# Edge attributes as three bf16 terms, in 24 one-pass products per step

## The chip, the cores and the metric

The kernel runs on one core of one Trainium2 chip. The metric is the device time of one execution in microseconds. A core has five engines that run their own instruction streams and meet only at semaphores: PE (TensorE, matrix products into the PSUM memory), DVE (VectorE), ACT (ScalarE), POOL (GpSimd) and SP (SyncE, which here only issues transfers). Transfers move on DMA queues: POOL issues the indirect ones (gathers of rows by index), SP and ACT the plain ones.

## The reference, cut to what matters

Four graph layers over 6,250 nodes with 96 features and 206,250 edges, sorted by destination. Every edge has 32 attributes. The two layers in the middle use them:

```python
# layer 1 (sum over the edges of a node)
msg = jax.nn.relu(x[src] + edge_attr @ We + be)
aggr = jax.ops.segment_sum(msg, dst, num_segments=x.shape[0])
...
# layer 2, twice (maximum over the edges of a node)
msg = x[src] @ W_msg + edge_attr @ W_edge
agg = jax.ops.segment_max(msg, dst, num_segments=x.shape[0])
return agg + x @ W_root + b
```

Layer 0 is an attention over edges in the other order (sorted by source), layer 3 an attention over the edges in the given order. Neither uses the attributes. All inputs are float32.

## The kernel before, in words

The program is a row of blocks, one after the other. A preparation block sorts and builds tables and loads the weights. Block `e0` is the attention stage of layer 0: 416 chunks of 512 edges. Three edge passes follow, all written by the same function `edge_pass`: `e1` (sum), `e2a` and `e2b` (maximum). Block `e3` is the attention of layer 3, 404 chunks of 512 edges in batches of four. Short node blocks stand between them.

**An edge pass** has 202 steps (`NS`), each of 1,024 edges that stand as 128 rows of 8 edges. For a step s:

- SP loads the attributes (`load_attr`, L1117), 128 rows of 256 float32: two blocks of 128 columns, four edges' 32 attributes each above one another on the rows. Four buffers (`RA`), so it runs four steps ahead; a load waits until PE is done with the buffer (`t_attr`). In even steps it loads masks, and then it stores the result of two steps earlier (L1126).
- POOL gathers the features of the 8 source nodes of each row by 8 indirect transfers (L1151) into one of three buffers. The gathers of step s + 3 wait until the `add` of step s has read its buffer (`v_add`).
- PE makes `edge_attr @ W` by two float32 products (L1168). The attributes are the operand that is held in the array (128x128), and the moving one is a 128x384 matrix with the 32x96 weight four times on its diagonal. Two PSUM buffers `EA`: the products of step s wait for the `add` of step s - 2. Every fourth step, PE also makes a transpose (L1166 in `e1`) or a product (L1164 in `e2a`, `e2b`) for one of the 49 node tiles, the "root" work.
- DVE waits for the products (`t_attr`) and the gathered rows and adds them (L1187), then transposes (L1193), runs three segmented scans (L1202) and transposes back (L1210). In `e1` ACT applies the relu (L1227) before the first transpose.

The last instruction of PE's step raises `t_attr`. Two instructions wait on it: DVE's `add(s)` and SP's attribute load of step s + 4.

**The attention stage `e0`**, per chunk: SP reads four row numbers from memory and issues four window loads (L766, L767), and stores an older chunk's result (L759). POOL makes four gathers (L789). DVE multiplies and reduces to scores (L877, L880), clips (L883), scans (L845) and multiplies by the weights (L894). ACT builds the selection matrices (L911, L914), takes the exponentials (L962, L964) and copies the result out of PSUM (L905). PE makes four float32 products for the queries (L805) and two groups of four transposes (L829, L812). The order of all of this is written out in the source, chunk by chunk.

## Time and profile before

| | |
|---|---|
| time, median of 3 executions | 13151.55 us (13120.66 to 13181.02) |
| span of the profiled execution, first to last instruction | 13179.5 us |
| that execution's own time, the highest of the three | 13181.02 us |
| PE busy, weight loads beside it | 4527.1 us (34%), 3022.1 us (23%) |
| DVE busy | 6535.8 us (50%) |
| ACT busy | 1994.5 us (15%) |
| POOL busy | 8151.7 us (62%) |
| attention stage `e0` | about 640 to 3,430 us |
| edge passes `e1`, `e2a`, `e2b` | about 3,440 to 5,712, 5,845 to 8,110, 8,210 to 10,480 us |
| attention `e3` | about 10,640 to 13,060 us |
| granted TensorE clock, mean | 0.541 of 2.4 GHz |

The table says how long each engine was at work, not who set the pace: no engine is busy for more than 62% of the span. That is read stage by stage, from what each engine waits for. Two things help to read the rows below. A float32 product stands in the trace as two MATMUL rows and two LDWEIGHTS rows (202 steps of two products give 808 of each). And the profile notes when a matrix product starts; its end is modelled. A wait that it puts down to "remote" or "issue" has no releaser that it could find.

### The profile page before, as it was taken

The numbers are of one execution on the slowest core, as the hardware profiler recorded it, in microseconds if no ns is written. First come the engines' busy times: TensorE is split into PE (matmuls) and PEld (weight loads), VectorE is DVE, ScalarE is ACT, GpSimd is POOL, SyncE is SP. The second block draws the span as 40 slices with busy tenths as digits, with TensorE's granted clock in tenths as the row PEclk, the third lists the DMA queues.
The fourth block names the chain that finished last, engine by engine and source line by source line (L and its number), as shares of the span: only waits on it lengthen the run. The fifth ranks groups of instructions, "written<-read, shape, count | busy, mean of one in ns | idle before, by whom it ended". The sixth has DMA issues, their size and how long they took to land. (4 is left out here: it accounts for less than half of the span.)

```text
span 13179.5 us, 81573 instructions
## 1 busy us (share of the span) xinstructions
PE 4527.1 (34%) x15877; PEld 3022.1 (23%) x15877; DVE 6535.8 (50%) x10237; ACT 1994.5 (15%) x4360; POOL 8151.7 (62%) x8551
## 2 busy tenths in 40 slices
PE   3354455555222222232222222222222234434443
PEld 3244344444110111111111111111111123333332
DVE  9543344444544454454445455444544544444445
ACT  3233333333100000010000000000000022222223
POOL 1455555555676666656666666766666666666665
PEclk7555555555555555555555555555555555555555
DMA  2355555555333333323333332333333222222222
GB/s 76 106 155 154 149 152 155 153 159 152 99 86 82 87 89 87 88 72 85 87 87 93 81 91 79 87 85 88 89 87 86 81 58 66 69 68 68 68 69 63
DMA packets 1007936, 1264.02 MB, mean 96 GB/s; under 512 B 483123, under 2 KB 740467, under 8 KB 1007331
## 3 DMA queue, kind: packets, MB, share of 16 engines
q0 software_dynamic: 303696, 520.91, 17.5%
q1 hardware_dynamic: 638139, 635.93, 14.8%
q10 hardware_dynamic: 65600, 101.96, 2.7%
q8 instruction: 136, 2.23, 0.1%
q14 instruction: 365, 2.99, 0.1%
HBM read 829.46 MB, written 428.44 MB: 95 GB/s over the span
## 5 line engine op out<-in xcount | busy, mean ns | idle before, releaser
L789 POOL DMA_INDIRECT e_got<-kv_tab,dst_cols x1661 | 1574.5, 948 | 1281.7 <-DVE e_pay L894 770.2
L1843 POOL DMA_INDIRECT e_got<-h_tab,src_tcols x1612 | 1540.9, 956 | 881.8 <-issue 473.8
L1151 POOL DMA_INDIRECT e2a_got<-x_tab,src_cols x1616 | 1531.3, 948 | 775.7 <-issue 556.2
L1151 POOL DMA_INDIRECT e_got<-x_tab,src_cols x1616 | 1553.5, 961 | 718.3 <-issue 586.9
L1151 POOL DMA_INDIRECT e2b_got<-x_tab,src_cols x1616 | 1531.3, 948 | 745.7 <-issue 518.8
L1168 PE MATMUL e2b_EA<-we_W_edge,e2b_attr 128*128 128x384 f32 x808 | 574.9, 866 | 1331.2 <-DVE e2b_emsg L1187 728.3
L1168 PE MATMUL e_EA<-we_We,e_attr 128*128 128x384 f32 x808 | 578.3, 871 | 1297.8 <-issue 898.1
L1168 PE MATMUL e2a_EA<-we_W_edge,e2a_attr 128*128 128x384 f32 x808 | 572.0, 862 | 1300.4 <-issue 767.3
L894 DVE TENSOR_TENSOR e_pay<-e_got,e_Q 128x384 f32<-128x384 f32 x416 | 230.2, 553 | 1570.4 <-ACT e_Q L962 1129.1
L1940 DVE TENSOR_TENSOR_SCAN e_run<-e_Z,e_run,e_msg 98x512 f32<-98x512 f32 x404 | 516.9, 1279 | 795.4 <-ACT e_msg L2005 619.8
L805 PE MATMUL e_Q<-e_window,e_pick 128*128 128x96 f32 x3328 | 758.9, 408 | 79.1 <-issue 41.2
L805 PEld LDWEIGHTS e_Q<-e_window,e_pick 128*128 128x128 f32 x3328 | 744.0, 327 | 84.8 <-issue 82.8
L812 PE MATMUL e_B<-ident,e_run 100*128 100x100 f32 x1664 | 374.5, 379 | 904.4 <-issue 493.3
L1854 PE MATMUL e_B<-ident,e_run 98*128 98x98 f32 x1616 | 357.1, 374 | 759.2 <-DVE e_run L1940 627.7
L1168 PEld LDWEIGHTS e2b_EA<-we_W_edge,e2b_attr 128*128 128x128 f32 x808 | 236.8, 323 | 1621.6 <-issue 1620.1
L829 PE MATMUL e_M<-ident,e_pay 128*100 128x128 f32 x1664 | 445.8, 422 | 470.0 <-DVE e_pay L894 366.4
L1168 PEld LDWEIGHTS e_EA<-we_We,e_attr 128*128 128x128 f32 x808 | 239.7, 327 | 1590.5 <-issue 1590.2
L1168 PEld LDWEIGHTS e2a_EA<-we_W_edge,e2a_attr 128*128 128x128 f32 x808 | 235.8, 321 | 1589.1 <-issue 1587.1
L845 DVE TENSOR_TENSOR_SCAN e_run<-e_keep,e_run,e_M 100x512 f32<-100x512 bf16 x416 | 532.3, 1280 | 11.5 <-issue 7.2
L1187 DVE TENSOR_TENSOR e2a_emsg<-e2a_EA,e2a_got 128x768 f32<-128x768 f32 x202 | 191.9, 950 | 692.4 <-remote 458.4
L1187 DVE TENSOR_TENSOR e2b_emsg<-e2b_EA,e2b_got 128x768 f32<-128x768 f32 x202 | 192.1, 951 | 671.5 <-remote 396.5
L1187 DVE TENSOR_TENSOR e_emsg<-e_EA,e_got 128x768 f32<-128x768 f32 x202 | 192.7, 954 | 648.3 <-remote 529.4
(373 smaller groups left out, 10316.0 us busy)
## 6 DMA issues: line engine op xcount, KB each, us to landing
scan_out<-e_out SPq DMA_DIRECT2D x416, 200.0 KB
e_window<-q_tab SPq DMA_DIRECT2D x1664, 48.0 KB
scan_out<-e_out SPq DMA_DIRECT2D x404, 196.0 KB
scan_out<-e_out SPq DMA_DIRECT2D x202, 384.0 KB
scan_out<-e2a_out SPq DMA_DIRECT2D x202, 384.0 KB
scan_out<-e2b_out SPq DMA_DIRECT2D x202, 384.0 KB
e_rel<-rel_row ACTq DMA_DIRECT2D x208, 256.0 KB
e_keep<-keep_row ACTq DMA_DIRECT2D x208, 200.0 KB
```

The costliest lines, as they stand in the source:

```text
L789: e.indirect_dma_start(got[i][:, k, :], None, kv_tab, bass.IndirectOffsetOnAxis(dst_c[:, c * K + k:c * K + k + 1], axis=0)).then_inc(s_g[i ...
L805: ins = e.matmul(Q[c % 3][:, k * D:(k + 1) * D], pick[c % 4][:, k, :], window[c % U][:, k, :], start=True, stop=True)
L812: ins = e.transpose(B[c % 2][:, k * PAY:(k + 1) * PAY], run[c % 3][:, k::K], ident[0:PAY, 0:PAY])
L829: ins = e.transpose(M[c % 3][0:PAY, k * P:(k + 1) * P], pay[c % 4][:, k, :], ident[:, :])
L845: e.tensor_tensor_scan(run[c % 3][:, :], keep[c // 2 % KR][:, at:at + CH], M[c % 3][0:PAY, :], run[(c + 2) % 3][:, CH - 1:CH], ALU.mult, A ...
L894: e.tensor_tensor(pay[c % 4][:, :, 0:D].rearrange("p k (h d) -> p k h d", h=HEADS), got[c % RG0][:, :, D:2 * D].rearrange("p k (h d) -> p ...
L1151: e.indirect_dma_start(got[s % RS][:, k, :], None, x_tab, bass.IndirectOffsetOnAxis(src_cols[:, q:q + 1], axis=0)).then_inc(edge_got[s % R ...
L1168: ins = e.matmul(EA[s % 2][:, h, 0:K * D], attr[s % RA][:, h * P:(h + 1) * P], edge_w[:, :], start=True, stop=True)
L1187: e.tensor_tensor(emsg[s % 3][:, :, :].rearrange("p (h k) d -> p h (k d)", h=2), EA[s % 2][:, :, 0:K * D], got[s % RS][:, :, :].rearrange( ...
L1843: e.indirect_dma_start(got[c % RG][:, k, :], None, h_tab, bass.IndirectOffsetOnAxis(src_tcols[:, q:q + 1], axis=0)).then_inc(s_g[c % RG], 16)
L1854: ins = e.transpose(B[v % 2][:, k * HW:(k + 1) * HW], run[v % 2][:, k::K], ident[0:HW, 0:HW])
L1940: V[v].give(e.tensor_tensor_scan(run[p][:, :], Z[p][0:HW, :], msg[p][:, :], run[q][:, CH - 1:CH], ALU.mult, ALU.add), "scan")
```

## The change

The attributes no longer stand as float32. In the attention stage `e0`, which does not use them, every batch of four steps' attributes (128 rows of 1,024) is loaded, split into three bf16 terms and stored in a table `attr_terms` in memory: the value rounded to bf16, the rest rounded to bf16, and the rest of that. The three add up to the float32 value. There are 51 batches, one every 8 chunks. SP loads a batch (L796) at chunk 2 of the eight, ACT rounds at chunks 3 and 5 (L1014, L1019), DVE subtracts at chunks 4 and 7 (L917, L922), SP stores the three terms at chunk 14 (three transfers, L802).

In the edge passes SP loads, for a step, the three terms one above the other: 96 rows of 1,024 bf16. The weights are split in the same way in the preparation block, each term standing three times on 96 rows. For each of a step's eight 128-edge columns, PE multiplies the same 96x128 attributes with the three terms of the weight and sums in PSUM. These are all nine pairs of terms. So a step's two float32 products with 384 moving columns become 24 bf16 products with 96 (L1254).

```diff
-        we = {n: keepb("we_" + n, [P, K * D]) for n in ("We", "W1_edge", "W2_edge")}
+        we = {n: keepb("we_" + n, [3 * DE, 3, D], BF16) for n in ("We", "W1_edge", "W2_edge")}
...
-                    e.wait_ge(p_set, 1 + len(we))
...
-                    for n in we:
-                        e.memset(we[n][:, :], 0.0).then_inc(p_set, 1)
...
+                    e.wait_ge(s_w, 16 * len(loads))
+                    for n in we:
+                        e.tensor_copy(we[n][:, 0, :], edge_f[n][:, :]).then_inc(p_edge, 1)
+                    e.wait_ge(p_edge, 3)
+                    for n in we:
+                        e.tensor_tensor(edge_f[n][:, :], edge_f[n][:, :], we[n][:, 0, :], ALU.subtract).then_inc(p_edge, 1)
...
+            SPLIT_AT, SPLIT_STEP = 2, 8
...
+                    def load_attr(b):
+                        n = split_rows(b)
+                        after(e, v_term, 2 * (b - 1))
+                        e.dma_start(attr_f[b % 2][0:n, :], t["attr_S"][b * P:b * P + n, :]).then_inc(s_af[b % 2], 16)
+
+                    def store_terms(b):
+                        n = split_rows(b)
+                        e.wait_ge(v_term, 2 * b + 2)
+                        for i in range(3):
+                            e.dma_start(attr_terms[b, i, 0:n, :], attr_t[b % 2][0:n, i, :]).then_inc(s_at[b % 2], 16)
...
+                    def rest(b):
+                        n = split_rows(b)
+                        e.wait_ge(a_term, 2 * b + 1)
+                        e.tensor_tensor(attr_f[b % 2][0:n, :], attr_f[b % 2][0:n, :], attr_t[b % 2][0:n, 0, :], ALU.subtract).then_inc(v_term, 1)
...
+                    def first_term(b):
+                        n = split_rows(b)
+                        e.wait_ge(s_af[b % 2], 16 * (b // 2 + 1))
+                        after(e, s_at[b % 2], 48 * (b // 2))
+                        e.activation(attr_t[b % 2][0:n, 0, :], attr_f[b % 2][0:n, :], ACT.Copy).then_inc(a_term, 1)
...
-                attr = [ph.sb(f"attr{i}", [P, 2 * P]) for i in range(RA)]
+                attr = [ph.sb(f"attr{i}", [3 * DE, 2 * K * P], BF16) for i in range(RA)]
...
                         def load_attr(s):
                             after(e, t_attr, s - RA + 1)
-                            e.dma_start(attr[s % RA][:, :], t["attr_S"][s]).then_inc(s_attr[s % RA], 16)
+                            lo = s % SPB * DE
+                            e.dma_start(attr[s % RA][:, :], attr_terms[s // SPB, :, lo:lo + DE, :]).then_inc(s_attr[s % RA], 16)
...
-                            for h in range(2):
-                                ins = e.matmul(EA[s % 2][:, h, 0:K * D], attr[s % RA][:, h * P:(h + 1) * P], edge_w[:, :], start=True, stop=True)
+                            for k in range(2 * K):
+                                for j in range(3):
+                                    ins = e.matmul(EA[s % 2][:, k // K, k % K * D:(k % K + 1) * D], attr[s % RA][:, k * P:(k + 1) * P], edge_w[:, j, :],
+                                                   start=j == 0, stop=j == 2)
                             ins.then_inc(t_attr, 1)
```

The order that stands in the built programs shows two places. The first is PE in the pass `e1`, one root step and the step behind it (`e_attr` are the attributes, `we_We` the weight). Before:

```order
L1166 MATMUL e_EA<-ident,X 96x128 [waits edge_v_pick,edge_v_add,edge_attr0]
L1168 MATMUL e_EA<-we_We,e_attr 128x384 x2
L1168 MATMUL e_EA<-we_We,e_attr 128x384 [waits edge_v_add,edge_attr1]
L1168 MATMUL e_EA<-we_We,e_attr 128x384
L1168 MATMUL e_EA<-we_We,e_attr 128x384 [waits edge_v_add,edge_attr2]
L1168 MATMUL e_EA<-we_We,e_attr 128x384
```

After:

```order
L1251 MATMUL e_EA<-ident,X 96x128 [waits edge_v_pick,edge_v_add,edge_attr0]
L1254 MATMUL e_EA<-we_We,e_attr 128x96 x24
L1254 MATMUL e_EA<-we_We,e_attr 128x96 [waits edge_v_add,edge_attr1]
L1254 MATMUL e_EA<-we_We,e_attr 128x96 x23
L1254 MATMUL e_EA<-we_We,e_attr 128x96 [waits edge_v_add,edge_attr2]
L1254 MATMUL e_EA<-we_We,e_attr 128x96 x23
```

The waits stand where they stood; a step has 24 instructions for 2.

The second place is SP in the attention stage, at a chunk where the terms of a batch are stored (`e_window` are the query rows, `R` holds a term). After:

```order
L810 DMA e_window<-q_tab 128x96
L791 DMA scan_out<-e_out 128x400 [waits edge_a_out]
L802 DMA attr_terms<-R 128x1024 [waits e0_g_v_term]
L802 DMA attr_terms<-R 128x1024 x2
L809 TENSOR_LOAD first_row [waits edge_t_q]
L809 ISA x2
```

Before:

```order
L767 DMA e_window<-q_tab 128x96
L759 DMA scan_out<-e_out 128x400 [waits edge_a_out]
L766 TENSOR_LOAD first_row [waits edge_t_q]
L766 ISA x2
```

Three stores, the first with a wait for DVE's last subtraction, now stand behind the store of a chunk and ahead of the next chunk's windows.

## Rows read from the trace of the kernel before

**Rows 1.** Windows of four stages; columns in the header row.
```profile
core 0: us, PE busy (x) PEld busy (x) DVE busy (x) ACT busy (x) POOL busy (x), PEclk, DMA share, GB/s
640.00:3430.00 2790.00, 1391.47 (x6270) 1204.76 (x6269) 1245.60 (x2061) 882.92 (x2143) 1560.32 (x1643) 0.51 0.55 151
3440.00:5712.00 2272.00, 588.77 (x857) 241.25 (x857) 1120.52 (x1258) 169.45 (x201) 1553.52 (x1616) 0.54 0.32 87
10640.00:13060.00 2420.00, 984.29 (x5376) 762.65 (x5377) 1143.52 (x2900) 620.95 (x1296) 1535.80 (x1608) 0.54 0.26 68
```

**Rows 2.** Source view of L1187, first pass: duration ns, first and last start.
```profile
L1187 DVE TENSOR_TENSOR e_emsg<-e_EA,e_got x202: 915/957/959, 3452.0 to 5711.5; 128x768 f32<-128x768 f32 x101
```

**Rows 3.** Costliest groups of the page (line, engine, names, busy, mean ns, idle, releaser).
```profile
L1151 POOL DMA_INDIRECT e_got<-x_tab,src_cols x1616 | 1553.5, 961 | 718.3 <-issue 586.9
L1168 PE MATMUL e_EA<-we_We,e_attr 128*128 128x384 f32 x808 | 578.3, 871 | 1297.8 <-issue 898.1
L1187 DVE TENSOR_TENSOR e_emsg<-e_EA,e_got 128x768 f32<-128x768 f32 x202 | 192.7, 954 | 648.3 <-remote 529.4
```

**Rows 4.** Timeline at 3494 us: start, duration, engine, line, operation, idle before.
```profile
3494.31 2.90 PE L1168 MATMUL e_EA<-we_We,e_attr 128*128 128x384 f32 x4 [8.55 <-issue]
3497.24 0.33 SPq L1117 DMA_DIRECT2D e_attr<-in_attr_S  x1
3501.66 0.96 DVE L1187 TENSOR_TENSOR e_emsg<-e_EA,e_got 128x768 f32<-128x768 f32 x1 [1.96 <-DMA e_got<-x_tab,src_cols]
```

**Rows 5.** Timeline at 4400 us, same pass.
```profile
4400.15 2.90 PE L1168 MATMUL e_EA<-we_We,e_attr 128*128 128x384 f32 x4 [8.28 <-issue]
...
4411.64 0.33 SPq L1117 DMA_DIRECT2D e_attr<-in_attr_S  x1
...
4413.07 0.94 POOL L1151 DMA_INDIRECT e_got<-x_tab,src_cols  x1 [3.11 <-issue]
...
4422.82 0.35 SPq L1117 DMA_DIRECT2D e_attr<-in_attr_S  x1
4422.83 0.96 DVE L1187 TENSOR_TENSOR e_emsg<-e_EA,e_got 128x768 f32<-128x768 f32 x1 [4.49 <-remote]
```

**Rows 6.** Timeline at 6420 us, second pass.
```profile
6420.26 0.33 SPq L1117 DMA_DIRECT2D e2a_attr<-in_attr_S  x1
...
6421.32 0.71 PE L1164 MATMUL e2a_EA<-Wrc,xT_all 96*128 96x96 f32 x2 [8.25 <-issue]
...
6431.46 0.35 SPq L1117 DMA_DIRECT2D e2a_attr<-in_attr_S  x1
...
6447.56 0.33 SPq L1117 DMA_DIRECT2D e2a_attr<-in_attr_S  x1
```

**Rows 7.** Timeline at 11580 us, attention over the ordered edges.
```profile
11576.14 1.06 PE L1868 MATMUL e_M<-ident,e_emsg 128*98 128x128 f32 x4
...
11584.15 0.94 POOL L1843 DMA_INDIRECT e_got<-h_tab,src_tcols  x1 [0.30 <-issue]
11587.67 0.60 ACT L2005 ACTIVATE e_msg<-e_M 98x512 f32<-98x512 f32 x1 [7.53 <-remote]
...
11589.34 0.95 POOL L1843 DMA_INDIRECT e_got<-h_tab,src_tcols  x1 [4.24 <-ACT e_hold L2017]
```

**Rows 8.** Timeline at 1490 us, first attention stage, SP's queue and POOL.
```profile
1486.81 10.37 SPq L767 DMA_DIRECT2D e_window<-q_tab  x4
...
1503.11 0.94 POOL L789 DMA_INDIRECT e_got<-kv_tab,dst_cols  x1 [8.20 <-DVE e_pay L894]
```

**Rows 9.** All groups by line: a bf16 product, and what bears on the split.
```profile
L1864 PE MATMUL e_Z<-e_parts,e_sel 80*98 80x128 bf16 x1616 | 252.2, 308 | 113.3 <-issue 74.0 <-DVE e_mid L1979 25.4 <-DVE e_parts L1981 10.5
L894 DVE TENSOR_TENSOR e_pay<-e_got,e_Q 128x384 f32<-128x384 f32 x416 | 230.2, 553 | 1570.4 <-ACT e_Q L962 1129.1 <-issue 440.8
L1227 ACT ACTIVATE e_emsg<-e_emsg 128x768 f32<-128x768 f32 x202 | 170.3, 843 | 2108.4 <-issue 1571.1 <-DVE e_emsg L1187 537.3
L647 DVE TENSOR_TENSOR prep_A<-prep_A 128x1024 f32<-128x1024 f32 x49 | 60.0, 1225 | 1.7
```

More of the change, by code:

```diff
@@ L147, in build @@
     neg_row = scratch("neg_row", (EP,), BF16)
+    SPB = P // DE
+    NAB = -(-(NCH // 2) // SPB)
+    attr_terms = scratch("attr_terms", (NAB, 3, P, 2 * K * P), BF16)
     ad_row = scratch("ad_row", (EP,))
@@ L335, in build @@
             assert NCH <= 512 and G * CH <= NT * D and NG <= PB
+            edge_f = {n: ph.sb("edge_f_" + n, [3 * DE, D]) for n in we}
+            p_edge = ph.sem("p_edge")
             loads = [(src_cols[:, 0:NCH * K], t["src_cols"]), (src_tcols[:, 0:NTL], t["src_tcols"])]
@@ L346, in build @@
             for n, key in (("We", "L1_gnn_We"), ("W1_edge", "L2_gnn_W1_edge"), ("W2_edge", "L2_gnn_W2_edge")):
-                for k in range(K):
-                    loads.append((we[n][k * DE:(k + 1) * DE, k * D:(k + 1) * D], t[key]))
+                for i in range(3):
+                    loads.append((edge_f[n][i * DE:(i + 1) * DE, :], t[key]))
             def pairs(buf, lo, n, y):
@@ L729, in build, with split_of, split_rows @@
             s_dst, v_keep, s_kept = pf.sem("dst"), pf.sem("keep"), pf.sem("st")
+            EW = 2 * K * P
+            assert 7 * EW // 2 <= NT * D
+            R_flat = R[:, :, :].rearrange("p t d -> p (t d)")
+            attr_f = [R_flat[:, i * EW:(i + 1) * EW] for i in range(2)]
+            attr_t = [R_flat[:, 2 * EW:7 * EW // 2].bitcast(BF16).rearrange("p (i n) -> p i n", i=3),
+                      pf.sb("attr_t1", [P, 3, EW], BF16)]
+            s_af, s_at = [ph.sem(f"g_af{i}") for i in range(2)], [ph.sem(f"g_at{i}") for i in range(2)]
+            a_term, v_term = ph.sem("g_a_term"), ph.sem("g_v_term")
+            SPLIT_AT, SPLIT_STEP = 2, 8
+            assert SPLIT_AT + SPLIT_STEP * (NAB - 1) + 12 < NCH0
+            def split_of(c, at):
+                b, r = divmod(c - SPLIT_AT - at, SPLIT_STEP)
+                return b if r == 0 and 0 <= b < NAB else None
+            def split_rows(b):
+                return min(P, NCH // 2 * DE - b * P)
             v_half, t_first, a_first, a_le, a_row, a_cnt, v_end = (pf.sem(n) for n in ("ld", "pe", "first", "le", "row", "cnt", "f"))
@@ L759, in store @@
                         e.dma_start(out_c[c], out[c % U][:, :, :].rearrange("p k d -> p (k d)")).then_inc(s_st[c % U], 16)
+                    def load_attr(b):
[5 more added lines that the diff above has]
+                        e.wait_ge(v_term, 2 * b + 2)
+                        for i in range(3):
+                            e.dma_start(attr_terms[b, i, 0:n, :], attr_t[b % 2][0:n, i, :]).then_inc(s_at[b % 2], 16)
                     BEHIND = 13
@@ L769, in _ @@
                             store(c - BEHIND)
+                        b = split_of(c, 0)
+                        if b is not None:
+                            load_attr(b)
+                        b = split_of(c, 12)
+                        if b is not None:
+                            store_terms(b)
                         if c == U - 1:
@@ L779, in _ @@
                     e.wait_ge(s_kept, 32)
+                    for i in range(2):
+                        e.wait_ge(s_at[i], 48 * len(range(i, NAB, 2)))
                     for u in range(U):
@@ L891, in _ @@
                             ends()
+                        b = split_of(c, 2)
+                        if b is not None:
+                            rest(b)
+                        b = split_of(c, 5)
+                        if b is not None:
+                            last_term(b)
                         e.wait_ge(a_exp, c + 1)
@@ L972, in _ @@
                             keep_in((c + 4) // 2)
+                        b = split_of(c, 1)
+                        if b is not None:
+                            first_term(b)
+                        b = split_of(c, 3)
+                        if b is not None:
+                            second_term(b)
                         if ROWS_AT <= c < ROWS_AT + NT:
```

17 lines of the change are left out of this document (16 added, 1 removed).

## The prediction, on record before the result

> **What bounds the kernel now.** I read the windows by stage first. In an edge pass no engine is full: DVE is busy for 1,120.5 of 2,272 us, POOL for 1,553.5, PE for 588.8 beside 241.3 of weight loads [rows 1]. So something waits. The source view of L1187, the addition at the head of DVE's step, gives the pace: 202 of them between 3452.0 and 5711.5 us [rows 2], 11.24 us a step. The other two passes have nearly the same length.
>
> POOL alone could go faster. A gather is 0.94 us, with 0.30 us of gap before it [rows 7], so eight take 10.0 us. DVE alone could go much faster: 1,120.5 / 202 is 5.5 us. In the page's costliest groups DVE idles 648 us before its addition, and the profile puts 529 of them down to "remote"; POOL idles 718 us [rows 3].
>
> The timeline tells who it is. Early in the pass (rows at 3494 us) a step's four MATMUL rows start at 3494.31 and last 2.90 us, and SP's attribute load, which waits for `t_attr` alone, starts at 3497.24: PE's word comes at once, and the addition waits for the gather until 3501.66 [rows 4]. Nine hundred microseconds later it is otherwise. The products of the step whose addition starts at 4422.83 stand in the trace at 4400.15, for 2.90 us. SP's load, which waits for the same `t_attr`, starts at 4422.82, within 0.01 us of the addition [rows 5]. At 4411.64 the load of the step before did the same. What DVE and SP have in common is `t_attr`, so the word of PE comes 19.8 us after the modelled end of its products. POOL is held by it in turn: it had been idle for 3.11 us at 4413.07 [rows 5]. **The late release by PE sets the pace of the edge passes**, and POOL's 10.0 us a step stands close below it.
>
> How long does it take per what? The loads are 11.18 us apart at 4411.64 and 4422.82 and 11.2 at 6420.26 and 6431.46, for four MATMUL and four LDWEIGHTS rows; in a step that holds the root product, with two rows of each more, 16.1 us (6431.46 to 6447.56; those products start at 6421.32) [rows 5, 6]. That is 1.4 us for each of 8 and 1.34 for each of 12 rows, though a root row has 96 columns and the others 384. So lateness goes by the number of instructions, not by columns.
>
> It is not always so dear. In the attention over the ordered edges 5,376 MATMUL and 5,377 LDWEIGHTS rows pass in 2,420 us, in the first attention stage 12,539 in 2,790 [rows 1]. But it is there too. Transposes at 11576.14 last 1.06 us and ACT, which waits for such transposes, starts at 11587.67, "remote"; POOL's last gather before it is at 11584.15, and POOL then idles 4.24 us [rows 7]. SP has its own form of it: four window loads that take 10.37 us, until POOL's stream stops for 8.20 us [rows 8]. What these have in common is a POOL that issues gathers without a break, and a backlog elsewhere that clears once it stops. I take this as the mechanism: while gathers stream, PE's completions get through slowly, and POOL's idle time is the price at which they clear.
>
> **The change part by part.** *The products.* Two float32 products become 24 bf16 ones. A bf16 product in the trace, 80x98 by 128 columns, is 308 ns from start to modelled end [rows 9]; if none overlapped, 24 would take 7.4 us, below POOL's 10.0. So the array's own work hides behind the gathers. The rows do not: 8 of them a step become 48, since each product brings a weight load though three in turn use the same one; the order shows no sharing. 202 x 40 is 8,080 more rows a pass.
>
> What is a row worth? I split the idle time of POOL into a share by gather and a share by PE row. Edge pass: (11.24 - 10.0) x 202 = 250 us for 1,616 gathers and 1,714 rows [rows 1, 2]. Last attention: 1,608 gathers at 1.25 us are 2,010 us of 2,420, leaving 410 us for 10,753 rows [rows 1]. The difference, 160 us for 9,039 rows, is 0.0178 us a row; a gather is then 0.136 us. The first attention stage tests it: 1,643 gathers at 1.25 are 2,054 of 2,790 us, 736 left; the two prices give 223 + 223 = 446. They fall short, and SP with some 21 instructions a chunk may be the rest. By 0.0178 us a pass gains 144 us of length, three passes 431 us, a step 11.95 us. If all that the first stage lacks is put on its rows, (736 - 223) / 12,539 = 0.041 us, a pass gains 331 us, three 993. Below stands zero, and a gain: if the lateness were gone altogether a pass would fall to POOL's 10.0 us a step, 606 x 1.24 = 751 us less; the pace at the pass's start, with 10.1, would give 691. I take 0.0178, the price between the two stages whose rows surround the new kernel's (8.5 and 107 rows to eight and sixteen gathers; it will have about 49 to eight).
>
> The Trainium skill has a rule that would put this lower: in "TensorE: Matmul & The Clock Gate" (LDWEIGHTS, Weight-path perf modes) a weight load costs its columns over the clock, less with fast weight load for bf16. By it the 24 weight loads would cost an estimated 2.6 us a step and be hidden, and the edge passes would end at POOL's pace. The trace agrees on the starts of the products and disagrees on their release, which is what others wait for.
>
> *The attribute load.* 96 rows of 2 KB for 128 rows of 1 KB, 192 KB for 128, one transfer as before, on a queue that has four steps (45 us) of lead. I cost it at nothing; if the lead were gone a step would wait for all of it. The trace shows no such transfer. The skill's "DMA: Bandwidth & Descriptors" (Why a DMA increments its semaphore by 16 and not by 1) says that the number of engines must divide the slowest dimension on both sides; with 3 terms on the source side that would be 3 engines, not 16. No row here shows that.
>
> *The split in the attention stage.* 51 batches. DVE: two subtractions of 128x1024, the like of which take 1.225 us [rows 9], 125 us in all. They stand ahead of L894, before which DVE idles 1,570 us in 416 chunks [rows 9], 3.8 us a chunk, so most is hidden. ACT: two copies of 128x1024, a third above the 0.843 us of 128x768 [rows 9], some 1.1 us each, 112 us in all; ACT is busy for 883 of 2,790 us [rows 1]. SP: four transfers a batch. SP's issue is near its limit here, with windows of 1 us at best and 2.6 us when they drag [rows 8]. At 0.5 us a transfer that is 102 us, at 2.6 us 530 us. Bounds: 0, were all hidden, and 125 + 112 + 530 = 767 us, were nothing hidden and every transfer dragged. I take 110 us: SP's four at the lower price, DVE and ACT hidden. The store's wait for DVE costs nothing by the order: SP's next windows wait for query products that PE makes after the DVE instruction in question. Behind it are only windows that could not start earlier.
>
> *The preparation.* Twelve small DVE instructions on 96 columns for three memsets, in a stage where DVE is nearly full: about 3 us.
>
> Sum: 13,179.5 + 431 + 110 + 3 = 13,724 us of span. The median of the runs shown is 29 us below the time of the profiled one, so 13,695 us; I say 13,700.
>
> **The rivals.**
>
> *A. The lateness goes.* If it belongs to float32 passes, and not to the number of rows, the passes run at POOL's 10.1 us: 13,152 - 691 + 113 = 12,570 us. For it: the pass starts that way, and for 110 us nothing is late [rows 4]. A bf16 row was never seen alone in a dragging stretch. Against it: transposes and SP's transfers are late too [rows 7, 8].
>
> *B. Rows keep the edge pass's price.* At 1.34 to 1.4 us each, 48 rows would take 64 to 67 us a step, 46 ms in all. Against it: the last attention would then take six times its time. A milder form is more likely: PE's backlog holds more than one step, each step waits until POOL has run out of buffers and paused, and a step takes 14 us: 606 x 2.76 = 1,673 us more, 14,900 us. It decides once two steps' rows (96) no longer clear in one pause of POOL. In the rows at 11580 us such a pause is 4.24 us for 16 gathers and over a hundred rows [rows 7].
>
> *C. The edge passes stay.* If what is late is set by the gathers and not by the rows, the step stays at 11.24 us and only the split is paid: 13,265 us, between 13,152 and 13,400 with its bounds.
>
> **How the numbers follow.** Forecast 0.45, A 0.31, B 0.12, C 0.12. Within the forecast the price of a row from 0.01 to 0.041 us gives 13,450 to 14,300. The whole range has to take in A, at 12,570, and reaches into B: 12,500 to 14,900. This kernel's executions spread by 0.5%, so 0.5%, 66 us, is about what can be told from no change. Faster by more than that: A and a sliver of the forecast, 0.32. Within: 0.07 of C's 0.12, and 0.01, together 0.08. Slower: the forecast, B and the rest of C, 0.60.
>
> **What would show it.** The additions of `e1` should be 11.9 us apart on average. SP's attribute load should still start together with the addition, long after the products' modelled end, and POOL should idle about 1.9 us a step. In the attention stage the chunks should grow from 6.7 to 7.0 us, with the growth at SP's queue. If the additions come every 10.1 us and wait for a gather, A is right and my reading of the rows at 11580 us was wrong. If POOL idles 4 us and more a step it is B. If the attention stage grows by more than 300 us, ACT or DVE was not covered.

## The result, and the profile after

| | before | after |
|---|---|---|
| time, median | 13139.25 us (13120.66 to 13181.02) | 13523.55 us (13507.21 to 13532.24) |
| ratio | | 1.0288, 95% interval 1.0273 to 1.0302 |
| span of the profiled execution | 13179.5 us | 13514.2 us |
| first to last scan of `e0` | 2870.7 us | 2961.1 us |
| first to last addition of `e1`, `e2a`, `e2b` | 2259.5, 2252.3, 2257.9 us | 2338.0, 2330.8, 2330.3 us |
| step of the edge passes | 11.2 us | 11.6 us |
| first to last scan of `e3` | 2406.3 us | 2412.9 us |

The changed kernel is 384 us slower by the medians; 549 us had been forecast. By the two profiled spans it is 335 us, and of these the table gives 90 us to the attention stage, 79, 79 and 72 us to the edge passes and 7 us to `e3`. The profiled execution of before was the slowest of its kind, so the spans show less than the medians.

The windows of the same three stages, with the columns of [rows 1]: `e0`, `e1`, `e3`.

```profile
core 0: us, PE busy (x) PEld busy (x) DVE busy (x) ACT busy (x) POOL busy (x), PEclk, DMA share, GB/s
640.00:3430.00 2790.00, 1363.73 (x6236) 1189.13 (x6236) 1291.07 (x2050) 967.15 (x2224) 1604.46 (x1598) 0.53 0.60 171
3550.00:5880.00 2330.00, 513.05 (x4838) 398.54 (x4837) 1100.84 (x1247) 168.26 (x200) 1515.10 (x1603) 0.50 0.32 90
10980.00:13400.00 2420.00, 998.54 (x5397) 770.16 (x5397) 1138.48 (x2902) 627.41 (x1303) 1525.73 (x1603) 0.53 0.26 68
```

In `e1` PE's products are busy for less than before (513 us for 589), with almost six times the instructions. The weight loads beside them grew from 241 to 399 us. Even together that is far below the 2,330 us of the stage: the array's work does not fill the step.

The source view of the addition, which is L1274 now, answers to [rows 2]:

```profile
L1274 DVE TENSOR_TENSOR e_emsg<-e_EA,e_got x202: 910/944/959, 3547.0 to 5885.0; 128x768 f32<-128x768 f32 x101
L1274 DVE TENSOR_TENSOR e2a_emsg<-e2a_EA,e2a_got x202: 910/932/959, 6032.5 to 8363.3; 128x768 f32<-128x768 f32 x101
L1274 DVE TENSOR_TENSOR e2b_emsg<-e2b_EA,e2b_got x202: 909/932/959, 8473.2 to 10803.5; 128x768 f32<-128x768 f32 x101
```

And the page's costliest groups answer to [rows 3]:

```profile
L1236 POOL DMA_INDIRECT e_got<-x_tab,src_cols x1616 | 1528.4, 946 | 819.5 <-issue 483.9
L1254 PE MATMUL e2a_EA<-we_W_edge,e2a_attr 96*128 96x96 bf16 x4848 | 517.9, 275 | 1624.3 <-issue 1551.6
...
L1254 PEld LDWEIGHTS e2a_EA<-we_W_edge,e2a_attr 96*128 96x128 bf16 x4848 | 405.8, 137 | 1735.1 <-issue 1734.0
...
L1274 DVE TENSOR_TENSOR e_emsg<-e_EA,e_got 128x768 f32<-128x768 f32 x202 | 189.2, 937 | 811.7 <-remote 787.5
```

POOL idles 819.5 us in `e1` for 718.3 before, DVE 811.7 us ahead of its addition for 648.3. A weight load is 137 ns, so the 24 of a step are 3.3 us. The Trainium skill, in "TensorE: Matmul & The Clock Gate" (LDWEIGHTS), puts a load at its columns over 1.2, in ns: an estimated 107 ns for 128 columns. The trace agrees roughly. The loads are short, but the step is longer all the same.

The timeline shows how a step waits. This is the stretch at 3649 us (start, duration, engine, line, operation, idle before), with one PE row shown where several are alike:

```profile
3649.17 0.71 SPq L1202 DMA_DIRECT2D e_attr<-attr_terms  x1
...
3649.39 0.94 DVE L1274 TENSOR_TENSOR e_emsg<-e_EA,e_got 128x768 f32<-128x768 f32 x1
...
3650.47 0.80 PE L1254 MATMUL e_EA<-we_We,e_attr 96*128 96x96 bf16 x8 [10.52 <-issue]
...
3652.27 2.02 DVE L1289 TENSOR_TENSOR_SCAN e_run<-e_mask,e_run,e_F 128x256 f32<-128x256 bf16 x3
...
3654.06 0.24 PE L1254 MATMUL e_EA<-we_We,e_attr 96*128 96x96 bf16 x1 [2.79 <-issue]
3654.32 1.55 DVE L1297 STREAM_TRANSPOSE e_out<-e_run 128x768 f32<-128x768 f32 x1
...
3663.16 0.24 PE L1254 MATMUL e_EA<-we_We,e_attr 96*128 96x96 bf16 x1 [2.56 <-issue]
...
3665.97 0.24 PE L1254 MATMUL e_EA<-we_We,e_attr 96*128 96x96 bf16 x1 [2.56 <-issue]
3666.67 0.10 PEld L1254 LDWEIGHTS e_EA<-we_We,e_attr 96*128 96x128 bf16 x1 [2.00 <-issue]
3667.37 0.24 PE L1254 MATMUL e_EA<-we_We,e_attr 96*128 96x96 bf16 x1 [1.16 <-issue]
3668.07 0.10 PEld L1254 LDWEIGHTS e_EA<-we_We,e_attr 96*128 96x128 bf16 x1 [1.30 <-issue]
3668.76 0.24 PE L1254 MATMUL e_EA<-we_We,e_attr 96*128 96x96 bf16 x1 [1.16 <-issue]
...
3669.46 0.24 PE L1254 MATMUL e_EA<-we_We,e_attr 96*128 96x96 bf16 x1 [0.46 <-issue]
...
3670.28 0.72 SPq L1202 DMA_DIRECT2D e_attr<-attr_terms  x1
3670.29 0.96 DVE L1274 TENSOR_TENSOR e_emsg<-e_EA,e_got 128x768 f32<-128x768 f32 x1 [14.42 <-remote]
...
3671.39 2.08 PE L1254 MATMUL e_EA<-we_We,e_attr 96*128 96x96 bf16 x24 [0.52 <-DVE e_emsg L1274]
3671.52 0.95 POOL L1236 DMA_INDIRECT e_got<-x_tab,src_cols  x1 [6.58 <-DVE e_emsg L1274]
```

Before, only the release was late and the products stood in the trace at once. Now the products themselves are spread out: eight start together at 3650.47, then one at a time, with starts about 0.70 us or two to four times that apart. At 3664.94 POOL runs out of free buffers and stops. PE's rows, products and weight loads taken together, then come every 0.70 us, and after 3670 all at once: 24 products in 2.08 us. DVE's instructions are not spread out in this way: its three scans at 3652.27 take 2.02 us together, and the transpose follows at once. SP's attribute load and the addition start together again, at 3670.28 and 3670.29. The next two additions follow 6.4 us apart (3670.29, 3676.72, 3683.10), and then it begins anew. Four steps take 46.3 us: 32 gathers of 1.25 us and one pause of POOL of 6.3 us more than its usual gap.

### The profile page after: what moved, and what is told of

The parts are those of the page before. It is cut to its first block and busy times, and to the rows that moved or that the text cites. A ratio compares the mean times of both kernels' runs of the same rounds, so it can differ in the third digit from the quotient of the medians.

```text
span 13514.2 us, 106279 instructions
## 1 busy us (share of the span) xinstructions
PE 4341.7 (32%) x27997; PEld 3517.6 (26%) x27997; DVE 6618.9 (49%) x10339; ACT 2093.7 (15%) x4462; POOL 8231.4 (61%) x8560
## 5 line engine op out<-in xcount | busy, mean ns | idle before, releaser
L840 POOL DMA_INDIRECT e_got<-kv_tab,dst_cols x1661 | 1670.3, 1006 | 1264.1 <-DVE e_pay L961 772.4
L1236 POOL DMA_INDIRECT e_got<-x_tab,src_cols x1616 | 1528.4, 946 | 819.5 <-issue 483.9
L1254 PE MATMUL e2a_EA<-we_W_edge,e2a_attr 96*128 96x96 bf16 x4848 | 517.9, 275 | 1624.3 <-issue 1551.6
L1254 PE MATMUL e2b_EA<-we_W_edge,e2b_attr 96*128 96x96 bf16 x4848 | 515.3, 275 | 1623.4 <-issue 1547.7
L1254 PE MATMUL e_EA<-we_We,e_attr 96*128 96x96 bf16 x4848 | 508.0, 275 | 1522.5 <-issue 1372.0
L1254 PEld LDWEIGHTS e2a_EA<-we_W_edge,e2a_attr 96*128 96x128 bf16 x4848 | 405.8, 137 | 1735.1 <-issue 1734.0
L1254 PEld LDWEIGHTS e2b_EA<-we_W_edge,e2b_attr 96*128 96x128 bf16 x4848 | 405.9, 137 | 1732.0 <-issue 1729.9
L961 DVE TENSOR_TENSOR e_pay<-e_got,e_Q 128x384 f32<-128x384 f32 x416 | 229.3, 551 | 1255.7 <-ACT e_Q L1040 840.0
L1254 PEld LDWEIGHTS e_EA<-we_We,e_attr 96*128 96x128 bf16 x4848 | 401.8, 137 | 1626.7 <-issue 1623.4
L1274 DVE TENSOR_TENSOR e_emsg<-e_EA,e_got 128x768 f32<-128x768 f32 x202 | 189.2, 937 | 811.7 <-remote 787.5
L1274 DVE TENSOR_TENSOR e2b_emsg<-e2b_EA,e2b_got 128x768 f32<-128x768 f32 x202 | 188.6, 933 | 797.9 <-remote 797.9
L1274 DVE TENSOR_TENSOR e2a_emsg<-e2a_EA,e2a_got 128x768 f32<-128x768 f32 x202 | 188.5, 933 | 789.1 <-remote 789.1
```

The lines of the kernel that those rows point to most:

```text
L840: e.indirect_dma_start(got[i][:, k, :], None, kv_tab, bass.IndirectOffsetOnAxis(dst_c[:, c * K + k:c * K + k + 1], axis=0)).then_inc(s_g[i ...
L961: e.tensor_tensor(pay[c % 4][:, :, 0:D].rearrange("p k (h d) -> p k h d", h=HEADS), got[c % RG0][:, :, D:2 * D].rearrange("p k (h d) -> p ...
L1236: e.indirect_dma_start(got[s % RS][:, k, :], None, x_tab, bass.IndirectOffsetOnAxis(src_cols[:, q:q + 1], axis=0)).then_inc(edge_got[s % R ...
L1254: ins = e.matmul(EA[s % 2][:, k // K, k % K * D:(k % K + 1) * D], attr[s % RA][:, k * P:(k + 1) * P], edge_w[:, j, :], start=j == 0, stop= ...
L1274: e.tensor_tensor(emsg[s % 3][:, :, :].rearrange("p (h k) d -> p h (k d)", h=2), EA[s % 2][:, :, 0:K * D], got[s % RS][:, :, :].rearrange( ...
```

## The experiments

The first four runs asked what sets the pace, and what the split costs apart from the passes.

**A third PSUM buffer for the products**, in both kernels:

```diff
-                EA = [ph.ps(f"EA{i}", [P, 2, CH]) for i in range(2)]
-                F = [ph.ps(f"F{i}", [P, 2 * CH]) for i in range(2)]
+                EA = [ph.ps(f"EA{i}", [P, 2, CH]) for i in range(3)]
+                F = [ph.ps("F0", [P, 2 * CH])]
...
-                            after(e, v_add, s - 1)
+                            after(e, v_add, s - 2)
...
-                            after(e, v_scan, s - 1)
-                            e.transpose(turned[s % 2], blocks(emsg[s % 3])).then_inc(v_fwd, 1)
+                            after(e, v_scan, s)
+                            e.transpose(turned[0], blocks(emsg[s % 3])).then_inc(v_fwd, 1)
...
```

> The kernel before with three PSUM buffers EA instead of two, and one buffer F instead of two, so that PE may run three steps ahead of the addition. Theory 1 (rows have a price: PE's work gets through at a limited rate while gathers stream, however far ahead it may run): the step stays at 11.2 us and the time at 13,140 us. Theory 2 (a fixed lateness: PE's word comes about 20 us after its products, and two buffers turn 20 us into 11.2 us a step): three buffers allow 7 us, so POOL's 10.1 us a step sets the pace, 606 x 1.1 = 670 us less, about 12,470 us.

> The changed kernel with the same third buffer EA. Theory 1 (rows have a price): the step stays at 11.6 us, the time near 13,520 us. Theory 2 (fixed lateness against two buffers): 10.1 us a step, 606 x 1.5 = 900 us less, about 12,620 us.

Measured: 13153.87 us against 13158.65 us for before, ratio 1.0003 (0.9988 to 1.0019), steps of 11.24, 11.23 and 11.23 us. On the changed kernel 13516.64 us, ratio to before 1.0282 (1.0241 to 1.0322), steps of 11.60, 11.59 and 11.61 us. Theory 2 is out. One step more that PE may run ahead changes nothing, so the lateness is not a fixed delay that the buffers divide.

**The split alone**, with the passes of before (shown against the changed kernel, which has the same split):

```diff
-                            lo = s % SPB * DE
-                            e.dma_start(attr[s % RA][:, :], attr_terms[s // SPB, :, lo:lo + DE, :]).then_inc(s_attr[s % RA], 16)
+                            e.dma_start(attr[s % RA][:, :], t["attr_S"][s]).then_inc(s_attr[s % RA], 16)
...
+                            for h in range(2):
+                                ins = e.matmul(EA[s % 2][:, h, 0:K * D], attr[s % RA][:, h * P:(h + 1) * P], edge_w[:, :], start=True, stop=True)
...
```

> The kernel before, with the split of the attributes in the attention stage and its stores as in the changed kernel; the edge passes still load float32 attributes and make two float32 products. If the split costs what the attention stage grew by (92 us between the first and the last scan), the time is 13,230 us and the edge passes are as before. If the split had also cost something later, or if the growth of that stage came from something else, it is off this by more than 40 us.

Measured: 13292.43 us, ratio 1.0101 (1.0070 to 1.0131), that is 134 us more, with 92 to 172 us inside the interval. The passes have 11.24, 11.22 and 11.23 us a step, as before. So the split is about a third of the loss, the new products are the rest. By the profile the attention stage has 2995.7 us from its first to its last scan here, 125 us more than before. One profile is a rough measure of this stage: in six kernels that leave it as it was it took 2844.5 to 2901.1 us.

**Where in the split**: all terms are computed, but only those of the last batch are stored.

```diff
-                        if b is not None:
+                        if b == NAB - 1:
                             store_terms(b)
...
```

> The kernel before with the split alone, as in the run before, but the three terms are stored for the last batch only (150 transfers of SP fewer; loads, ACT's copies and DVE's subtractions stay). The split as a whole cost 134 us. If, as I put it in the prediction, SP's transfers are what costs (three of the four of a batch are stores), some 100 us go: 13,170 us. If ACT's and DVE's work is what costs, nearly all stays: 13,270 us.

Measured: 13372.04 us against 13248.59 us for before on the same chip, ratio 1.0091 (1.0074 to 1.0108), some 120 us. 150 transfers less took nothing away that can be told. The groups show what is left (the lines are the changed kernel's): DVE's two subtractions are 51 of 1.22 us and 51 of 1.20 us, 123 us. The time that DVE idles ahead of its multiplication did fall, from 1570.4 us [rows 9] to 1255.7 us, and I had counted on that. But DVE now idles ahead of the subtraction instead, for ACT:

```profile
L961 DVE TENSOR_TENSOR e_pay<-e_got,e_Q 128x384 f32<-128x384 f32 x416 | 229.3, 551 | 1255.7 <-ACT e_Q L1040 840.0 <-issue 412.3 <-remote 3.2
...
L917 DVE TENSOR_TENSOR R<-R,find_attr_t 128x1024 f32<-128x1024 f32 x25 | 30.6, 1225 | 146.3 <-ACT find_attr_t L1014 146.3
L917 DVE TENSOR_TENSOR R<-R 128x1024 f32<-128x1024 f32 x25 | 30.6, 1224 | 138.3 <-ACT R L1014 133.1 <-issue 5.1
L922 DVE TENSOR_TENSOR R<-R 128x1024 bf16<-128x1024 f32 x25 | 30.0, 1200 | 0.0
L922 DVE TENSOR_TENSOR find_attr_t<-R,find_attr_t 128x1024 bf16<-128x1024 f32 x25 | 30.0, 1200 | 0.0
...
L1014 ACT ACTIVATE find_attr_t<-R 128x1024 bf16<-128x1024 f32 x25 | 26.0, 1039 | 0.0
```

1255.7 + 146.3 + 138.3 is 1540.3 us, against 1570.4: idle time that moved, not idle time that was used. In the run without the stores the three are 1367.5, 114.2 and 105.6 us, together 1587.3. DVE stands in the loop of the stage: POOL's gathers wait for its multiplication (before and after, some 770 us of POOL's idle time are put down to it), and the multiplication now stands behind the subtraction. So DVE's subtractions can lengthen the loop. That they alone do is not shown. The sum says where DVE's time went, not what caused it. ACT's copies, about 106 us (51 batches of two at 1.04 us), are in the same loop, for DVE waits for ACT ahead of its multiplication and ahead of the first subtraction, and no run has the one without the other, or without the load of the batch.

**The number of PE rows**, with the steps of all three passes below. One term of the weights, 8 products of 96 columns:

```diff
-                                for j in range(3):
+                                for j in range(1):
...
-                                                   start=j == 0, stop=j == 2)
+                                                   start=j == 0, stop=True)
```

> The changed kernel with the first term of the weights alone: 8 bf16 products a step instead of 24 (16 PE rows instead of 48; the result lacks the smaller terms of the weights). Theory 1 with a price in proportion to the number of rows (0.37 us a step for 40 rows more): 11.3 us a step, 13,350 us. Rival (float32 products are what is dear, bf16 rows are nearly free until their number is large): 10.1 us a step, 12,630 us.

Two bf16 products of 384 columns:

```diff
-                            for k in range(2 * K):
-                                for j in range(3):
-                                    ins = e.matmul(EA[s % 2][:, k // K, k % K * D:(k % K + 1) * D], attr[s % RA][:, k * P:(k + 1) * P], edge_w[:, j, :],
-                                                   start=j == 0, stop=j == 2)
+                            for h in range(2):
+                                ins = e.matmul(EA[s % 2][:, h, 0:K * D].rearrange("p (k d) -> p k d", k=K), attr[s % RA][:, h * P:(h + 1) * P], edge_w[:, 0:1, :].to_broadcast([3 * DE, K, D]), start=True, stop=True)
```

> The changed kernel with 2 bf16 products of 384 columns a step instead of 24 of 96 (4 PE rows a step instead of 48; every edge of a step gets the products of two of its columns, so the result isn't the reference's). Price by rows, from the steps measured so far (8.5 rows 11.23 us, 16.5 rows 11.36, 48.5 rows 11.60): 11.15 us a step, 13,250 us with the split. Rival (lateness is a debt that only begins above some rows per step): with a quarter of the changed kernel's columns and a twelfth of its rows the passes run at POOL's 10.1 us, 12,620 us.

The float32 products of before, twice:

```diff
-                            for h in range(2):
+                            for h in [0, 1] * 2:
```

> The kernel before with its two float32 products made twice into the same place (16 PE rows a step instead of 8). Price by rows, as in the run with 8 bf16 products: 11.35 us a step, 13,220 us. Rival (a float32 row costs its 1.4 us, as the 16 steps of 0.70 us between two releases suggest): 22 us a step, 19,600 us.

The 24 bf16 products twice:

```diff
-                                for j in range(3):
+                                for j in [0, 1, 2] * 2:
```

> The changed kernel with its 24 products made twice into the same place (96 PE rows a step). Price by rows at 0.008 us, the slope from 16 to 48 rows: 12.0 us a step, 13,750 us. Rival (backlog: two steps' rows no longer clear in a pause of POOL): 14 us a step or more, 14,900 us. PE's own work is some 5 us a step and hides in either.

| kernel | PE rows of the products a step | step of `e1`, `e2a`, `e2b`, us | time, us | ratio to before |
|---|---|---|---|---|
| 2 bf16 products, 384 columns | 4 | 11.14, 11.14, 11.15 | 13295.71 | 1.0121 (1.0099 to 1.0143) |
| before | 8 | 11.24, 11.21, 11.23 | 13139.25 | 1 |
| 8 bf16 products, 96 columns | 16 | 11.30, 11.39, 11.39 | 13378.35 | 1.0174 (1.0133 to 1.0214) |
| 4 float32 products, 384 columns | 16 | 11.37, 11.34, 11.36 | 13238.19 | 1.0059 (1.0036 to 1.0081) |
| 24 bf16 products, 96 columns | 48 | 11.63, 11.60, 11.59 | 13523.55 | 1.0288 (1.0273 to 1.0302) |
| 48 bf16 products, 96 columns | 96 | 11.93, 11.96, 11.96 | 13797.47 | 1.0501 (1.0483 to 1.0519) |

(The times of all but before and the float32 products hold the split.) The step grows with the number of rows, at a rate that falls slightly: by the means of the three passes 0.021 us a row from 4 to 8, 0.017 from 8 to 16, 0.0077 from 16 to 48, 0.0071 from 48 to 96. From 8 to 48 it is 0.38 / 40 = 0.0095 us. Type and columns do not show at 16 rows: float32 with 384 columns and bf16 with 96 columns both take 11.36 us a step in the mean, although the granted clock was 0.600 in the one and 0.520 in the other. The same pair differs in the attribute load, 96 rows of 2 KB for 128 rows of 1 KB. Unless two effects cancel, it costs nothing. The Trainium skill says in "DMA: Bandwidth & Descriptors" (Why a DMA increments its semaphore by 16 and not by 1) that the number of engines divides the slowest dimension on both sides, which makes 3 here. How many there were no row shows, and no cost of it could be measured.

All four rivals of these runs are out: float32 rows are not what is dear, no step fell to 10.1 us with 4 rows, a row does not cost 1.4 us, and 96 rows do not lead to a backlog of 14 us a step.

The kernel with 4 rows shows something else. These are the first five of eight gathers in a row there, out of a stretch in which they drag:

```profile
4413.20 1.09 POOL L1236 DMA_INDIRECT e_got<-x_tab,src_cols  x1 [0.30 <-issue]
...
4414.60 1.09 POOL L1236 DMA_INDIRECT e_got<-x_tab,src_cols  x1 [0.30 <-issue]
4415.14 0.84 ACT L1312 ACTIVATE e_emsg<-e_emsg 128x768 f32<-128x768 f32 x1 [7.40 <-DVE e_emsg L1272]
...
4415.99 1.10 POOL L1236 DMA_INDIRECT e_got<-x_tab,src_cols  x1 [0.30 <-issue]
...
4417.40 1.11 POOL L1236 DMA_INDIRECT e_got<-x_tab,src_cols  x1 [0.31 <-issue]
4418.81 1.09 POOL L1236 DMA_INDIRECT e_got<-x_tab,src_cols  x1 [0.30 <-issue]
```

and its source and group views of the gathers:

```profile
L1236 POOL DMA_INDIRECT e_got<-x_tab,src_cols x1616: 943/952/2259, 3534.2 to 5784.9; - x180
...
L1236 POOL DMA_INDIRECT e2a_got<-x_tab,src_cols x1616 | 1718.5, 1063 | 586.9 <-issue 532.6 <-ACTq L1196 54.3
```

DVE holds POOL no longer (no idle time is put down to it). PE's release is prompt: its products end at 4430.05 by the model and SP's load, which waits for it, starts at 4430.08. The addition waits for gathers:

```profile
4429.25 0.80 PE L1253 MATMUL e_EA<-we_We,e_attr 96*128 96x384 bf16 x2 [13.20 <-issue]
...
4430.08 0.71 SPq L1202 DMA_DIRECT2D e_attr<-attr_terms  x1
...
4436.23 0.96 DVE L1272 TENSOR_TENSOR e_emsg<-e_EA,e_got 128x768 f32<-128x768 f32 x1 [1.58 <-DMA e_got<-x_tab,src_cols]
```

Yet the step is 11.14 us, because the gathers themselves drag. In about a third to a half of the cases the next one comes after 1.40 us, twice the 0.70 us of PE's rows, and about one gather a step takes longer still. Their mean is 1063 ns in `e2a`, for 946 in the changed kernel and 948 before. **With 8 gathers a step no kernel ran below 11.1 us for long, though POOL alone would need 10.0.** In the kernel before the gathers do not drag; there POOL pauses for DVE, and the pace is nearly the same. That one limit stands behind both is likely and not shown. The 10 us a step at the start of a pass hold for its first 19 steps in `e1`, here and in the kernel before, and for 15 in `e2a` and `e2b` of the kernel before.

**One gather fewer:**

```diff
-                            for k in range(2 * K):
+                            for k in range(2 * K if s < RS else 2 * K - 1):
...
-                            e.wait_ge(edge_got[s % RS], got_before[s % RS] + 32 * K * (s // RS + 1))
+                            e.wait_ge(edge_got[s % RS], got_before[s % RS] + 32 * K + 16 * (2 * K - 1) * (s // RS))
...
```

> The kernel before with 7 instead of 8 gathers a step from the fourth step on (the eighth row of every group keeps its first content, so the result isn't the reference's). If POOL's idle time is a price by PE row and gather added to POOL's own work, a step falls by one gather, 1.25 us, and a little idle: 9.9 us, 13,140 - 606 x 1.35 = 12,320 us. If instead PE's rows set the pace by themselves, at 0.70 us a tick, 16 ticks a step, the step stays at 11.2 us, POOL idles 2.4 us a step, and the time stays at 13,140 us.

Measured: 12330.49 us, ratio 0.9369 (0.9348 to 0.9390), steps of 9.87 us in all three passes. PE's rows set no pace of their own at 11.2 us; a gather takes 1.36 us of a step with it.

**Half the bytes of each gather:**

```diff
-                                e.indirect_dma_start(got[s % RS][:, k, :], None, x_tab,
+                                wd = D if s < RS else D // 2
+                                e.indirect_dma_start(got[s % RS][:, k, 0:wd], None, x_tab if wd == D else x_tab.rearrange("n (h d) -> (n h) d", h=2),
```

> The kernel before with gathers of 192 bytes a row instead of 384 in the edge passes, from the fourth step on (same number of gathers and of rows; half of each row keeps its first content, so the result isn't the reference's). With 4 PE rows a step the passes still took 11.14 us a step, 1.39 us a gather, with POOL never held by DVE. If the bytes of the gathers make 1.39 us out of 1.25, a step falls to 10.1 to 10.4 us: 12,460 to 12,650 us. If it is their number, nothing changes: 11.2 us, 13,140 us.

Measured: 13250.83 us against 13248.59 us, ratio 0.9999 (0.9990 to 1.0009), steps of 11.26, 11.22 and 11.24 us. The bytes of a gather do not matter.

**Half of the gathers**, with the 24 products:

```diff
-                            for k in range(2 * K):
+                            for k in range(2 * K if s < RS else K):
...
-                            e.wait_ge(edge_got[s % RS], got_before[s % RS] + 32 * K * (s // RS + 1))
+                            e.wait_ge(edge_got[s % RS], got_before[s % RS] + 32 * K + 16 * K * (s // RS))
...
```

> The changed kernel with 4 of the 8 gathers a step from the fourth step on (the result isn't the reference's). Price by gather and by row (1.39 us x 4 + 48.5 x 0.0085): 6.0 us a step in the maximum passes; the sum pass has its own chain of DVE and ACT at 6.4 us: 13,524 - 202 x 5.2 - 404 x 5.6 = 10,210 us. If rows are free once POOL has slack, the maximum passes run at DVE's 5.5 us: 10,010 us. If PE's rows, at 0.70 us a tick, set a pace of their own, the step stays above 10 us: over 12,600 us.

Measured: 10458.25 us, ratio 0.7890 (0.7877 to 0.7903), steps of 6.52, 6.22 and 6.18 us. The sum of the prices gave 6.0 us for the maximum passes; 0.2 us are missing, and the whole kernel is 248 us above what I expected. Part of that is this chip, on which before takes 13248.59 us, 109 us more than in the first comparison. The third theory (over 12,600 us) is out, the second (5.5 us a step) too: the step stays above DVE's 5.5 us and above POOL's own work, 5.0 us. What the 1.2 us beyond POOL's work are made of is not shown, for no kernel with four gathers has fewer rows.

**Instructions on another engine**, 40 tiny ones a step on ACT in the two maximum passes, where it has no other work:

```diff
+                    if not relu:
+                        spare, a_spare = ph.sb("spare", [D, 40]), ph.sem("a_spare")
...
+                            for s in range(NS):
+                                e.wait_ge(v_add, s + 1)
+                                after(e, a_spare, s)
+                                for i in range(40):
+                                    ins = e.activation(spare[:, i:i + 1], mean_m[:, 0:1], ACT.Copy)
+                                ins.then_inc(a_spare, 1)
```

> The kernel before with 40 tiny ACT instructions (96x1) a step in the two maximum passes, where ACT is otherwise idle: as many instructions more as the changed kernel has PE rows more. If the price of 0.009 us belongs to any instruction beside a stream of gathers: 404 x 40 x 0.009 = 150 us more, 13,290 us, with both passes at 11.6 us a step and the sum pass at 11.2. If it belongs to PE's rows alone: 13,140 us and 11.2 us a step.

Measured: 14444.54 us, ratio 1.0899 (1.0881 to 1.0917). Both expectations missed. The passes keep their pace (11.27, 11.19, 11.17 us a step), but the run puts fewer instructions beside the gathers than it was meant to: in `e2a` 1,888 of the 8,080 start before the last gather, 9 a step and not 40. Nine a step at 0.0095 us would be 0.09 us a step, and no such growth is seen; what 40 a step would cost is not shown. And each pass ends some 600 us late, for ACT is not done: the last addition of `e2a` starts at 8143.6 us, the first of `e2b` at 8867.4 us. Two windows of that kernel, one inside the pass and one behind its last gather:

```profile
7000.00:7500.00 500.00, 128.83 (x193) 54.79 (x193) 240.70 (x271) 71.72 (x411) 329.51 (x350) 0.53 0.32 85
8300.00:8500.00 200.00, 0.00 (x0) 0.00 (x0) 0.00 (x0) 195.11 (x2032) 0.00 (x0) 0.50 0.00 1
```

ACT starts 411 instructions in 500 us inside the pass, 0.8 a microsecond, and 2,032 in 200 us behind it, 10 a microsecond. Inside the pass seven start at once, and then they stand on a grid like PE's:

```profile
7010.93 0.76 ACT L1231 ACTIVATE e2a_spare<-mean_m 96x1 f32<-96x1 f32 x7 [9.67 <-remote]
...
7012.25 0.20 ACT L1231 ACTIVATE e2a_spare<-mean_m 96x1 f32<-96x1 f32 x1 [0.56 <-issue]
...
7013.65 0.20 ACT L1231 ACTIVATE e2a_spare<-mean_m 96x1 f32<-96x1 f32 x1 [1.20 <-issue]
...
7014.36 0.20 ACT L1231 ACTIVATE e2a_spare<-mean_m 96x1 f32<-96x1 f32 x1 [0.51 <-issue]
7015.06 0.20 ACT L1231 ACTIVATE e2a_spare<-mean_m 96x1 f32<-96x1 f32 x1 [0.50 <-issue]
```

The second window has no gathers, but no work of PE and DVE either. The end of the pass tells them apart:

```profile
8140.98 0.94 POOL L1151 DMA_INDIRECT e2a_got<-x_tab,src_cols  x1 [0.30 <-issue]
...
8147.69 1.55 DVE L1210 STREAM_TRANSPOSE e2a_out<-e2a_run 128x768 f32<-128x768 f32 x1
...
8151.18 0.20 ACT L1231 ACTIVATE e2a_spare<-mean_m 96x1 f32<-96x1 f32 x1 [1.20 <-issue]
...
8156.07 9.09 ACT L1231 ACTIVATE e2a_spare<-mean_m 96x1 f32<-96x1 f32 x92 [0.50 <-issue]
```

The last gather starts at 8140.98 and DVE is done at 8149.24, yet ACT stays on the grid until 8156.07 and is then fast at once. So the slow rate is no property of PE, and it does not need PE, DVE or POOL at work at that moment. It outlasts the gathers by some 14 us, as PE's outlasted POOL's stop at 3664.94 by 5 us, as if something filled up during the stream and took time to empty. And it does not touch every engine, for DVE's few instructions a step follow one another without gaps.

## Why the prediction was right, and where it was off

- *The direction and the range*: slower, 13523.55 us, within 12,500 to 14,900, and by 384 us where 549 were forecast.
- *The products: what is paid for is the number of PE rows, not the array's time nor the columns.* Shown for these edge passes, by the table of six kernels, and by `e1`, where the products were busy for less and the step took longer.
- *The price of a row.* This is the term that was mis-sized. Forecast were 0.0178 us a row, 0.71 us a step, 431 us; measured 0.0095 us, 0.38 us a step, 229 us by the spans of the three passes. The step that failed is the comparison with the attention over the ordered edges: I put all of POOL's idle time there, beyond a share by gather, on PE's rows, and took the mean between 8.5 and 107 rows for the price of the 40 that were added. The view of all groups names who released POOL, and I had passed it over. It is the same in both kernels, here the one before:

```profile
L1843 POOL DMA_INDIRECT e_got<-h_tab,src_tcols x1612 | 1540.9, 956 | 881.8 <-issue 473.8 <-ACT e_hold L2017 398.7 <-POOLq L1596 9.0
```

  The gaps of 0.30 us are the 473.8 us; of what is left, the 410 us that I had shared out, 398.7 are waits for ACT, which copies the gathered tiles out. With 0.0095 us for each of the 10,753 rows and 0.136 for each of the 1,608 gathers, 321 of the 410 us come out, and some 90 are left over. What makes ACT late there was not tried, so this explanation of the size is argued, not shown. The price for a gather, from the same split, came out well: 0.136 us beyond its 1.25, and 8 x 0.136 + 10.0 = 11.1 us, which is the step with four rows.
- *"The late release by PE sets the pace, and POOL's 10.0 us stands close below it".* Half wrong. PE's release was late, but most of the 1.24 us above 10.0 do not hang on it. With prompt releases the step is still 11.14 us, for the gathers themselves drag. The four rows that before has more account for the last 0.09 us. The forecast did not depend on this, rival A did.
- *Rival A* (10.1 us a step, 12,570 us, 0.31): not to be had at 8 gathers a step, not even with 4 rows. Its weight was too high, since I took the start of a pass for a pace that can be kept.
- *Rivals B and C*: 96 rows still take 11.95 us, so there is no such backlog up to twice the change; and the passes did not stay at 11.24 us.
- *The attribute load*: forecast at nothing, and no cost could be seen.
- *The split*: forecast 110 us, measured 134 us (92 to 172) alone, 90 and 125 us by the spans. The size was right, and that was luck, for the reason was wrong. SP's transfers, on which I had put all of it, cost nothing measurable in their greater part, the stores. What is left is DVE's 123 us and ACT's 106 us, both of which I had called hidden, and the loads; the parts were not tried one by one. The idle time ahead of an instruction in a loop is not room.
- *The sum*: for a price of 0.01 us a row I named 13,450 us as the lower end. My own terms give 13,152 + 242 + 113 = 13,507 us. The measured price, 0.0095 us, lies just below that end of the prices, and the time, 13523.55 us, just above that end of the times, for the split was a little dearer than its 110 us.
- *The markers*: additions 11.6 us apart for the 11.9 named; SP's load together with the addition, as named; POOL idle for 6.3 us once in four steps, 1.6 us a step, for the 1.9 named; chunks of the first stage from 6.9 to 7.1 us, a growth of 0.2 for 0.3, and, as far as the stores go, not at SP's queue.

Open: what engines and gathers share. The runs show a grid of 0.70 us, or twice that, on PE, ACT and POOL, and not on DVE. Seven or eight instructions still start at once before it (ACT at 7010.93, PE at 3650.47). It begins only after a stream has gone on: 15 to 19 steps with 8 rows a step, about four with 16, and within the first with 48. It ends some time after POOL has stopped. They don't show what fills up. Every execution timed here was also recorded instruction by instruction, so they can't tell whether the recording has a part in it. Nor do they show why the first rows cost more than the later ones, or what the missing 0.2 us with four gathers are.

## What to carry to other kernels

Beside a long stream of indirect gathers, count PE's instructions, not its work: going from 2 long products to 24 short ones cost 0.4 us a step with the products less busy than before. The lever is the number of gathers (1.36 us of every step each), not a third PSUM buffer, the bytes of a gather or PE's time. And before idle time is called cover, ask whether the idle engine stands in the loop that sets the pace: where the added work is waited for by the same consumers, its idle time only moves.

## What the runs showed of the hardware that I had not expected

- A gather of 128 rows is issued every 1.25 us at first and costs 1.39 us in a long run (11.14 us for eight, with 4 PE rows a step). Whether a row has 384 or 192 bytes makes no difference (ratio 0.9999).
- While gathers streamed, ACT started 0.8 tiny instructions a microsecond, and 10 from 14 us after the last gather's end; PE's rows and the dragging gathers kept to the same grid of 0.70 us, and DVE's instructions did not.
- The 9 such instructions a step that ACT got done beside the gathers did not slow them (11.19 us a step), while 40 PE rows more made it 11.6. PE's rows are waited for in every step, ACT's were not; that this is the reason is a guess.
